# Token biases of two attention layers moved from GpSimd and VectorE into TensorE's products

## The reference, cut to what matters

```
# layer 2: softmax of q over the head's columns, of k over the tokens
xn = layernorm(x);  q = xn @ Wq + bq;  k = xn @ Wk + bk;  v = xn @ Wv + bv
k = where(mask == 1, -inf, k);  v = where(mask == 1, 0, v)
y = q (k^T v) per head;  h = silu(layernorm(y) * (1 + scale) + shift) @ film_out_W + film_out_b
x = x + h
# layer 3: softmax attention over 1024 keys, 16 heads of 16 columns
q = xn @ q_w + q_b;  k = xn @ k_w + k_b;  v = (xn @ v_w + v_b) * mask
y = softmax(q k^T + mask) v;  h = silu(layernorm(y) * (1 + scale) + shift) @ out_w + out_b
x = x + h
```

## Time and the profile before

| | us |
|---|---|
| median of 3 runs | 2312.39 (2309.84 to 2314.17) |
| time of the profiled execution | 2308.6 |
| its span, first to last instruction | 2306.9 |
| PE, DVE, ACT, POOL busy | 1935.9, 1880.3, 1191.2, 1205.0 |

### The profile page before, as it was taken

The page is one execution under the profiler, slowest core; times in us unless marked ns, Lnnn a source line. Parts: engine busy times, 40 slices in busy tenths (PEclk is TensorE's granted clock), DMA queues, the critical chain, the costliest instruction groups (busy, mean ns, idle before and its releaser), DMA issues.

```text
span 2306.9 us, 19180 instructions
## 1 busy us (share of the span) xinstructions
PE 1935.9 (84%) x5976; PEld 783.4 (34%) x5976; DVE 1880.3 (82%) x2184; ACT 1191.2 (52%) x2127; POOL 1205.0 (52%) x596
## 2 busy tenths in 40 slices
PE   6787998979898888878787888797776779999986
PEld 2232433324242323333332323243653323333323
DVE  2667989889898999899998999899657598888823
ACT  2635464455555656545455555553341236666673
POOL 2566867768787877767787776677212100000000
PEclk8799999989999999989999999999896779999998
DMA  5141122112222222212222222322041052221001
GB/s 191 47 135 61 64 66 66 59 60 73 66 69 70 77 70 73 70 56 65 71 71 70 78 68 70 104 69 78 1 96 15 0 113 31 29 35 24 2 2 37
DMA packets 80996, 144.36 MB, mean 63 GB/s; under 512 B 14616, under 2 KB 19672, under 8 KB 80358
## 3 DMA queue, kind: packets, MB, share of 16 engines
q1 hardware_dynamic: 80894, 143.14, 21.9%
HBM read 133.50 MB, written 9.01 MB: 62 GB/s over the span
## 4 chain that ended last, share of the span: by engine, by line
PE 50%; DVE 25%; POOL 11%; issue 7%; ACT 5%; DMA 1%; SPq 1%; DVEq 0%; POOLq 0%; ACTq 0%
PE psum L1578 14%; DVE hbuf L2123 11%; POOL hbuf L1330 8%; PE psum L698 5%; PE psum L1417 5%; DVE hbuf L2108 4%; PE psum L684 4%; DVE gain L970 4%; PE psum L664 4%; PE psum L580 3%; PE psum L1558 2%; PE psum L1393 2%; PE psum L1571 2%; PE psum L1441 2%; PE psum L570 2%
## 5 line engine op out<-in xcount | busy, mean ns | idle before, releaser
L1330 POOL TENSOR_TENSOR hbuf<-hbuf,cbuf 128x1024 f32<-128x1024 f32 x384 | 903.6, 2357 | 402.5 <-ACT hlast L1936 197.4
L1578 PE MATMUL psum<-hbuf,ident 128*128 128x512 f32 x1536 | 792.9, 640 | 127.3 <-POOL hbuf L1330 127.1
L1928 ACT ACTIVATE psum<-slots,cols 128x512 f32<-128x512 f32 x768 | 524.0, 686 | 454.4 <-DVE hbuf L2123 451.4
L2108 DVE TENSOR_TENSOR hbuf<-slots,psum 128x1024 f32<-128x1024 f32 x384 | 461.1, 1201 | 100.0 <-PE psum L1558 51.9
L2123 DVE TENSOR_TENSOR_SCAN hbuf<-psum,hlast,hbuf 128x512 f32<-128x512 f32 x384 | 470.9, 1269 | 13.6 <-ACT psum L1928 13.6
L2123 DVE TENSOR_TENSOR_SCAN hbuf<-psum,hbuf 128x512 f32<-128x512 f32 x384 | 447.6, 1207 | 18.9 <-ACT psum L1928 18.9
L1578 PEld LDWEIGHTS psum<-hbuf,ident 128*128 128x128 f32 x1536 | 273.4, 196 | 448.6 <-issue 270.6
L970 DVE TENSOR_REDUCE gain<-psum 128x1 f32<-128x512 f32 x512 | 314.7, 682 | 72.5 <-PE psum L664 72.1
L664 PE MATMUL psum<-slots 99*128 99x512 bf16 x512 | 211.9, 417 | 32.2 <-DVE gain L970 19.1
L684 PE MATMUL psum<-slots 102*128 102x512 bf16 x512 | 195.1, 389 | 6.4 <-ACT xn_flat L848 1.7
L1558 PE MATMUL psum<-bcs,pick 48*128 48x512 bf16 x384 | 153.1, 399 | 56.5 <-DVE hbuf L2108 54.1
(11 more groups left out here) (257 smaller groups left out, 2001.7 us busy)
## 6 DMA issues: line engine op xcount, KB each, us to landing
cbuf<-scr_c SPq DMA_DIRECT2D x384, 256.0 KB, 3.1
slots<-scr_qk SPq DMA_DIRECT2D x96, 128.0 KB
scr_qk<-slots SPq DMA_DIRECT2D x10, 512.0 KB, 2.8
wl<-in_w SPq DMA_DIRECT2D x1, 3968.0 KB, 12.4
wl<-in_ada_w SPq DMA_DIRECT2D x1, 3584.0 KB
xt<-in_x SPq DMA_DIRECT2D x2, 1024.0 KB, 12.4
wl<-in_w SPq DMA_DIRECT2D x2, 1024.0 KB, 6.9
out<-xt SPq DMA_DIRECT2D x2, 1024.0 KB, 4.4
```

Source lines behind the costliest of these rows:

```text
L1330: pool.tensor_tensor(hs, hs, cbuf[:, at % CRING:at % CRING + 1, :].to_broadcast([P, 2, TC]), ALU.mult).then_inc(weighed, 1)
L1578: last = pe.matmul(psum[:, q, :], ident[:, :], hbuf[:, at % RING, q, :], start=False, stop=n == NS - 1, skip_group_check=True)
L1928: act.activation(decay_bank(at, q), dts[k % 2][:, e, :], ACT.Exp, scale=coefficient(WORK[k], e, n)).then_inc(decay, 1)
L2108: dve.tensor_tensor(hbuf[:, at % RING, :, :], ws[k % 2][:, 2 * p:2 * p + 2, :], psum[:, 2 + at % 2:3 + at % 2, :].to_broadcast([P, 2, TC]) ...
```

## The change

1. The biases of "2q", "2v", "3v", "2out" and "3out" are no longer added by an instruction of their own. `to_tokens` (and the products of batch 0 in `attention_inputs`) begins each group with one bf16 matmul of K = 3 rows, `ones` [3,128] by `bias_rows` [3, 2 x 256], which writes the bias to the whole bank; the fp32 matmuls add to it. There are 10 such products of 4 groups, so 40 matmuls more.
2. `bias_rows` holds the six rows of 256 columns as three bf16 parts on three partitions. `split_biases` makes it on VectorE behind `beside(-1)`, with seven instructions over 3x1536.
3. The masks of v come in with the eviction: `masked_out` takes a group with two ACT instructions of 128x256, whose scale is the mask's column.
4. GpSimd keeps the memsets and the copies of `fill_quad`. The waits on `v_ready`, `v3_ready`, `ob_added` and `q_shifted`'s addition are gone; `turn_keys(0)` waits for the eviction of "2v".
5. ScalarE's order: three of the `deviation` calls stand two groups earlier ("2q" of batch 1, "2kT" of batch 1, "3v" of batch 0).
6. The broadcast load of `rows` has 768 columns in place of 1792, its two reloads in the last chunk are gone, and one load of 3x1536 is added at the start.

```diff
-            def to_tokens(name, b, src, w):
+            def to_tokens(name, b, src, w, bias):
                 for pair in range(TT // 2):
                     ps = start(name, b, pair)
+                    pe.matmul(ps, ones[:, :], bias_of(bias), start=True, stop=False, skip_group_check=True)
                     for q in range(2):
...
                             last = pe.matmul(ps[:, q * D:(q + 1) * D], src[:, k, t0:t0 + P], w[:, k, :],
-                                             start=k == 0, stop=k == KD - 1)
+                                             start=False, stop=k == KD - 1, skip_group_check=True)
...
+        def masked_out(act, ps, dst, pair, mask, b):
+            for q in range(2):
+                i = 2 * pair + q
+                last = act.activation(dst[:, i, :], ps[:, q * D:(q + 1) * D], ACT.Identity, scale=mask[:, b * TT + i:b * TT + i + 1])
+            return last
...
-            tokens_out("2q", 1, L2[1].q)
+            tokens_out("2q", 1, L2[1].q, (0, 1))
             deviation()
+            tokens_out("2q", 1, L2[1].q, (2, 3))
...
-            tokens_out("3v", 0, v3[0])
+            values_out("3v", 0, v3[0], m3c, (0, 1))
             deviation()
+            values_out("3v", 0, v3[0], m3c, (2, 3))
...
             def shift_queries(b):
                 m = L2[b]
-                link(dve.tensor_tensor(m.q, m.q, per_column(bq2), ALU.add))
...
-            pool.wait_ge(keep_ready, 1)
-            pool.wait_ge(ld_rows, 48)
-            finish_v2(0)
-            add_out_bias(1, 0, ob2)
-            add_out_bias(2, 1, ob2)
-            finish_v2(1)
-            finish_v3(0)
-            add_out_bias(3, 0, ob3)
             pool.wait_ge(qk_split, 1)
...
+            def split_biases():
+                hi, mid, low = bias_parts
+                dve.wait_ge(ld_bias, 16)
+                link(dve.tensor_copy(hi, bias_raw))
+                link(dve.tensor_tensor(bias_rest, bias_raw, hi, ALU.subtract))
+                link(dve.tensor_copy(mid, bias_rest))
+                dve.tensor_scalar(bias_rows[:, :], hi, ident[0:3, 0:1], None, ALU.mult)
+                link(dve.tensor_tensor(low, bias_rest, mid, ALU.subtract))
+                link(dve.scalar_tensor_tensor(bias_rows[:, :], mid, ident[0:3, 1:2], bias_rows[:, :], ALU.mult, ALU.add))
+                dve.scalar_tensor_tensor(bias_rows[:, :], low, ident[0:3, 2:3], bias_rows[:, :], ALU.mult, ALU.add).then_inc(bias_ready, 1)
+                dve.wait_ge(bias_ready, 1)
...
             for _ in beside(-1):
                 pass
+            split_biases()
             dve.wait_ge(mask_stored, 48 * BATCH)
             load(0)
```

More of the change, by code:

```diff
@@ L42 @@
 NCOLS = 286
-R_G0, R_B0, R_G1, R_B1, R_G2, R_B2, R_BF = 0, 256, 512, 768, 1024, 1280, 1536
-NROWS = 1792
+R_G1, R_B1, R_BF, NROWS = 0, 256, 512, 768
+BQ2, BV2, OB2, BV3, OB3, NBIAS = range(6)
 ADA = [768, 768, 512, 512]
@@ L295, in build @@
         bc_mid = hflat[RANK:XP, 2 * SEQ + SEQ // 2:3 * SEQ].bitcast(BF16)
+        bias_raw, bias_rest = (hflat[0:3, SEQ + n * NBIAS * D:SEQ + (n + 1) * NBIAS * D] for n in range(2))
+        bias_parts = [hflat[0:3, SEQ + (4 + n) * NBIAS * D // 2:SEQ + (5 + n) * NBIAS * D // 2].bitcast(BF16) for n in range(2)]
+        bias_parts += [hflat[0:3, SEQ:SEQ + NBIAS * D // 2].bitcast(BF16)]
         w_in = w0s[:, W0_IN:W0_XP].rearrange("p (k m) -> p k m", k=KD)
@@ L424, in build, with bias_of @@
         inv3 = head_scale[:, :].rearrange("p (i h) -> p i h", i=TT)
-        bq2, bv2, ob2 = (rows[:, n * D:(n + 1) * D] for n in range(3))
-        bv3, ob3 = (rows[:, n * D:(n + 1) * D] for n in (3, 4))
+        def bias_of(n):
+            return bias_rows[:, n * D:(n + 1) * D].rearrange("p (o d) -> p o d", o=1).to_broadcast([3, 2, D])
+        def masked_out(act, ps, dst, pair, mask, b):
[3 more added lines that the diff above has]
+            return last
         def tokens_of_batch(b):
@@ L491, in sync_attention, with pool_attention @@
                     load_stack(job + QUADS)
[L493 to L514, removed]
+        def pool_attention(pool):
             def fill_quad(job):
                 b, quad = job // QUADS, job % QUADS
-                pool.wait_ge(v3_ready, b + 1)
+                pool.wait_ge(t_act, t_taken(("3v", b, 3)))
                 if job >= 2:
@@ L587, in turn_keys @@
             def turn_keys(b):
+                if b == 0:
+                    pe.wait_ge(taken_act, taken(G["2v", 0, 3]))
                 pe.wait_ge(kn_ready, b + 1)
@@ L621, in attend, with film @@
                     last.then_inc(t_done, 1)
-            def film(name, n, b, h, hT, w):
+            def film(name, n, b, h, hT, w, bias):
                 pe.wait_ge(h_ready, n)
@@ L626, in film @@
                 after_act(name + "hT", b, 3)
-                to_tokens(name + "out", b, hT, w)
+                to_tokens(name + "out", b, hT, w, bias)
             def turn_x3(b):
@@ L1528, in attention_inputs @@
                 pe.wait_ge(taken_act, taken(G["2xT", 0, 3]))
-                for name, at, wn in (("2q", 13, w[:, 0]), ("2v", 18, w[:, 2])):
+                pe.wait_ge(bias_ready, 1)
+                for name, at, wn, bias in (("2q", 13, w[:, 0], BQ2), ("2v", 18, w[:, 2], BV2)):
                     for i in range(4):
                         ps = begin(name, 0, i)
+                        pe.matmul(ps, ones[:, :], bias_of(bias), start=True, stop=False, skip_group_check=True)
                         for q in range(2):
@@ L1826, in attention_inputs @@
                                    scale=cols[:, C_N + k:C_N + k + 1], bias=cols[:, C_N + KD + k:C_N + KD + k + 1]).then_inc(taken_act, 1)
[L1827 to L1830, removed]
-                                       ACT.Identity).then_inc(taken_act, 1)
+                for i in range(4):
+                    yield 14 + i
+                    act.activation(m.q[:, 2 * i:2 * i + 2, :], take("2q", 0, i).rearrange("p (q d) -> p q d", q=2),
+                                   ACT.Identity).then_inc(taken_act, 1)
+                act.wait_ge(keep_ready, 1)
+                for i in range(4):
+                    yield 19 + i
+                    masked_out(act, take("2v", 0, i), m.v, i, keep2, 0).then_inc(taken_act, 1)
                 for i in range(4):
```

70 lines of the change are left out of this document (32 added, 38 removed).

## The result

The changed kernel takes 2288.64 us (median of 4 runs, 2285.53 to 2293.82) against 2313.28 for the kernel before (4 runs); the ratio is 0.990, 95% interval 0.9882 to 0.9917. That is 24.6 us faster; 28.3 had been worked out, 2284 forecast. The profiled execution took 2285.53, its span is 2283.7, 23.2 less than before. A copy run later on another chip gave 0.9917 (0.9900 to 0.9933), with executions from 2286.4 to 2294.1.

What follows compares the result with a forecast made beforehand. It took the attention layers up to the first maximum as a chain of small stages that the biases lie on or hold up. Terms summing to 28.3 us took 2308.6 to 2280.3; 3.8 for the median gave 2284, range 2272 to 2296.

Steps and rivals of the forecast that it cites:

- The end of the scans: VectorE loses one bias instruction and two others run unslowed by GpSimd, so TensorE's last projection comes earlier: 9.5 us won.
- the deviation of "2kT": In "2kT" VectorE's layernorm waits 3.90 us for ScalarE's deviation, which moves up by two groups: 3.3 us won.
- the wait for v: TensorE no longer waits for GpSimd's two instructions on v: 6.4 us, plus 2.6 for the clock, 9.0 won.
- the price of "2v": In "2v" of batch 1, four bias matmuls and 0.2 us for the last group's two-instruction eviction: 1.45 us lost.
- the film of batch 1: From "3v" to "2out" of batch 1, the layernorm takes 2.7 us, not 16.09, and "2out" begins earlier: 15.7 us won.
- `split_max`: In the first job, two VectorE instructions of 2.85 and 3.71 us fall to at most 0.3 each: 6.0 us won.
- the price of a bias matmul: On TensorE, 0.31 us each, bounds 0 and 0.62, so 12.4 us for all 40, spread over the other terms.
- the low clock: Half the "2out" clock losses won back (1.2 and 1.25 us); rival that the clock stays low: 2287 to 2299, chance 0.17.
- The prediction's own sign: In the new profile, 0.31 us from a bias matmul to the next; a step far from that would prove it wrong.
- The start: VectorE's split_biases, taking turns with GpSimd, delays the first slot and all that follows: 9.6 us lost, lower bound 4.8.
- The first rival: At the start VectorE isn't held by GpSimd, or later slots take some up: 4.8 to 9.6 us better, chance 0.2.
- the early deviations: ScalarE's deviation calls two groups earlier: 3.3 us won at "2kT"; at "2q" 3.5 less 0.6 for two bias matmuls.

Runs made afterwards that it cites:

- gpsimd_busy: Changed kernel plus eight idle GpSimd instructions of 128x768, started by the last group of 2y of batch 1; 2290.66 us in one execution.
- before_gpsimd_out: Kernel before without GpSimd's twelve instructions for bv, the masks of v and the out biases, those biases and masks left out; 2276.57 us, ratio 0.9847.
- no_bias_mm: Changed kernel without its 40 bias matmuls, so without the five token biases; 2266.21 us (median of three), ratio 0.9803.
- two_bias_mm: Changed kernel with every bias matmul issued twice, one behind the other; 2304.81 us, ratio 0.9969.
- deviations_alone: Kernel before with only the three deviation calls moved two groups earlier in ScalarE's order; 2286.6 us, ratio 0.9893.
- early_film: Changed kernel with split_biases ahead of beside(-1) and the out products' bias matmuls issued ahead, while TensorE waits for hT; 2274.53 us, ratio 0.9839.
- ahead_and_early: Changed kernel with split_biases ahead of beside(-1), out products' bias matmuls issued ahead, and the attention layers' other bias matmuls in twos; 2277.0 us, ratio 0.9855.

## Why the prediction was right, and where it was off

The time lay in the range and the direction held; 28.3 us had been worked out for the profiled execution, and 23.2 came. Two errors of size lie behind that, 8 us one way and 2.6 the other; that the total misses by 5 and not by 8 is luck. By its steps:

The gains hold one by one. The end of the scans gave 9.6 (9.5), the deviation of "2kT" 3.3 (3.3), the wait for v, with the clock, 8.7 (9.0), which less the price of "2v" is 6.7 (7.55), the film of batch 1 14.7 (15.7), `split_max` 6.1 (6.0). gpsimd_busy shows the mechanism behind three of them, before_gpsimd_out most of their sum, 33.5 us with the biases left out.

The term that was mis-sized is the price of a bias matmul. It was taken from the spread, which is followed by fp32 but whose own start behind fp32 I didn't look at; only the step after it (0.31) was read. The trace of the kernel before had the whole price, one slot ahead of the earlier trace rows:

```profile
1560.11 0.39 PE L1558 MATMUL psum<-bcs,pick 48*128 48x512 bf16 x1
1560.42 1.98 PE L1578 MATMUL psum<-hbuf,ident 128*128 128x512 f32 x4
1562.24 1.89 PE L1535 MATMUL psum<-wl 128*128 128x256 f32 x8
```

From this spread to the next at 1564.07 it is 3.96 us. Four fp32 instructions of 128x512 take 1.72 where they follow their like (L570), eight of 128x256 take 1.73 (L580), which leaves 0.51 for the spread. In the changed kernel the pitch of a group shows 0.51, no_bias_mm 0.50, two_bias_mm that 0.3 of it is the place between fp32 matmuls. Over 40 the missing 0.2 is 8 us, which is why 28.3 was too much. It was inside the bound of 0.62, but that bound stood for the low clock, and 0.51 was measured at the full one. The prediction's own sign, 0.31 from a bias matmul to the next, came out as stated up to the fp32 matmul behind it, and so could not show the error.

The start was sized at 9.6 and cost 7.0. The mechanism is the one forecast, turns with GpSimd. Of the 2.6 that it was too large, 1.3 come from the rows, taken as 1536 and really 1280 (8.3 us of own work in place of 9.6), 1.0 from GpSimd, which held the seven instructions for 3.9 us (12.2 less 8.3) and not 4.9, and the rest from L2018, which ended some 0.4 earlier. The first rival, a cheaper start, has its two halves: that VectorE isn't held falls, that later slots take some of it up isn't excluded, up to some 2 us.

The low clock came in part. "2out" of batch 0 stayed at the full level, where the forecast had counted half of that gain; the first group of "2out" of batch 1 did not (3.44 for eight instructions in place of 1.99, at a granted clock of 0.61 from 1732 to 1736), and the projections of layer 3 lost 1.8 (L550 took 15.83 and L570 before 14.00; the clock was 0.53 from 1794 to 1798), which no step had. The loop of layer 3 was 1.5 longer, but in the copy it took 416.3 us, as in the kernel before (416.4; 417.9 in the changed one), so that is scatter between executions.

What the prediction didn't see is how the gain is shared. It gave the early deviations 3.3 and some 3, and the 13.4 of the layernorm to GpSimd's absence. deviations_alone and before_gpsimd_out show that either one is enough, for all of the 13.4 or for 11.6 of it: with the calls early, the layernorm is through before GpSimd starts. So a gain as large as the whole change's was to be had without moving any bias, and what the biases' move adds beyond that (9.6, 8.7 and 6.1) was paid back by 20 us of matmuls and 7 at the start. early_film takes back what can be hidden of these.

## What to carry to other kernels

Before work is moved off an engine that holds another up, see which of the two starts first: a small instruction queued behind evictions can decide whether a whole layernorm runs before or inside the hold. A short bf16 matmul cost more than twice its columns between fp32 ones here; read such a price from group to group, never from one start to the next, and put it where TensorE waits anyway. Preparation belongs to the idle stretch ahead of the first critical instruction, not just ahead of that instruction.

## What the runs showed of the hardware that was not expected

A bf16 matmul with K = 3 and 512 columns costs 0.51 us alone between fp32 matmuls of 128x256, at the full clock (2.24 less 1.73), and 0.22 behind another bf16 one (2.46 less 2.24); with K = 48 the price is the same 0.51 (the spread, in the kernel before). In ahead_and_early the scans lost about 6 us more over a stretch of 300 than in the changed kernel, at a lower granted clock, with the same instructions; spreads of this size between executions hide a few us of any change, and marks behind the scans are the way around that.
